# Who rounds the gate, who splits the last weights, and who makes the second products in a quantised feed-forward layer

## The reference, cut to what matters

```python
def act_qdq(x):                       # 16-bit rounding, scale from the largest value
    scale = jnp.maximum(jnp.max(jnp.abs(x)) / 32767, 1e-12)
    return jnp.clip(jnp.round(x / scale), -32768, 32767) * scale
x = act_qdq(x)
up = act_qdq(x @ lpbq_dequant(w_up).T)
gate = act_qdq(x @ lpbq_dequant(w_gate).T)
sig = fixed_qdq_u16(jax.nn.sigmoid(gate))    # round(s * 65536) / 65536
gate = act_qdq(gate * sig)
o = act_qdq(gate * up)
return o @ lpbq_dequant(w_down).T
```

## Time and profile before

| what | us |
|---|---|
| median of 3 runs (lowest, highest) | 802.72 (801.65, 803.15) |
| the profiled execution's own time | 802.26 |
| its span | 800.4 |
| gate matmuls, in the trace | about 541.9 to 613 |
| first loop, until its last product is done | about 614.5 to 683.1 |
| second loop, until its last maximum | about 685.9 to 730.6 |
| down matmuls to the end | about 733.5 to 798 |

### The profile page before, as it was taken

The page is one execution under the profiler, slowest core; times in us unless marked ns, Lnnn a source line. Parts: engine busy times, 40 slices in busy tenths (PEclk is TensorE's granted clock), DMA queues, the critical chain, the costliest instruction groups (busy, mean ns, idle before and its releaser), DMA issues.

```text
span 800.4 us, 11827 instructions
## 1 busy us (share of the span) xinstructions
PE 681.0 (85%) x4160; PEld 462.0 (58%) x4160; DVE 613.7 (77%) x1219; ACT 503.2 (63%) x682; POOL 312.4 (39%) x250
## 2 busy tenths in 40 slices
PE   6882059999999888999999999999998999008998
PEld 5761037988888754566556656564443445004887
DVE  5988866877787388887767675988998899896433
ACT  2235614444553437796896886776665999796983
POOL 4353612566777544233422420002440444694000
PEclk9997559999999999999999999999999999558999
DMA  9937633467634470010013000001100613101343
GB/s 297 339 95 262 194 103 120 122 174 175 146 66 53 107 249 1 2 48 27 1 49 132 1 27 27 27 27 55 78 26 1 237 53 132 52 0 53 113 153 106
DMA packets 59541, 78.68 MB, mean 98 GB/s; under 512 B 7904, under 2 KB 47712, under 8 KB 59488
## 3 DMA queue, kind: packets, MB, share of 16 engines
q1 hardware_dynamic: 49936, 61.10, 23.1%
q0 software_dynamic: 7872, 14.82, 8.5%
q10 hardware_dynamic: 1680, 2.08, 0.8%
HBM read 50.59 MB, written 27.39 MB: 97 GB/s over the span
## 4 chain that ended last, share of the span: by engine, by line
PE 57%; DVE 15%; ACT 13%; issue 4%; POOL 2%; DMA 1%; POOLq 0%; ACTq 0%; DVEq 0%
PE bank L2423 11%; PE bank L2134 8%; PE bank L2190 7%; PE bank L2454 5%; PE bank L1479 4%; PE bank L1513 3%; PE bank L1536 3%; PE bank L1573 3%; PE bank L1533 3%; DVE above L796 2%; PE bank L1494 2%; ACT wgateT L2083 2%; PE bank L1517 2%; DVE high L1914 1%; DVE qx L1208 1%
## 5 line engine op out<-in xcount | busy, mean ns | idle before, releaser
L1334 ACT ACTIVATE x<-bank,bic 128x512 f32<-128x512 f32 x160 | 106.3, 698 | 34.0 <-PE bank L1513 32.6
L1208 DVE TENSOR_REDUCE qx<-bank 128x4 fp32r<-128x616 f32 x128 | 98.2, 797 | 26.9 <-PE bank L1479 25.5
L2134 PE MATMUL bank<-ux,uwh 128*128 128x512 f16 x384 | 92.1, 382 | 0.4 <-ACT ux L2028 0.3
L2134 PEld LDWEIGHTS bank<-ux,uwh 128*128 128x128 f16 x384 | 37.6, 98 | 46.5 <-issue 1.9
L1513 PE MATMUL bank<-qT,K 128*128 128x512 f32 x128 | 61.4, 490 | 3.5 <-ACT x L1334 2.1
L2384 ACT ACTIVATE wgateT<-bank 128x512 f32<-128x512 f32 x32 | 19.2, 600 | 66.1 <-PE bank L2423 66.1
L1479 PE MATMUL bank<-Kb,qTb 128*128 128x308 bf16 x256 | 53.3, 298 | 4.9 <-DVE qx L1208 2.2
L1135 POOL CAST qx<-q 128x1024 fp32r<-128x1024 f32 x8 | 8.5, 1067 | 113.0 <-PE bank L1494 104.0
L2423 PE MATMUL bank<-xh,wh 128*128 128x512 f32 x128 | 50.2, 392 | 0.3 <-DVE xl L2357 0.3
L2134 PE MATMUL bank<-ux,uwl 128*128 128x512 f16 x192 | 50.1, 384 | 0.0
L2423 PE MATMUL bank<-xl,wh 128*128 128x512 f32 x128 | 49.9, 390 | 0.0
(11 more groups left out here) (440 smaller groups left out, 1992.0 us busy)
## 6 DMA issues: line engine op xcount, KB each, us to landing
x_dram<-x SPq DMA_DIRECT2D x4, 1024.0 KB, 5.7
xr<-in_w1T SPq DMA_DIRECT2D x8, 512.0 KB, 4.0
xr<-in_w3T SPq DMA_DIRECT2D x8, 512.0 KB, 4.8
xr<-in_w2T SPq DMA_DIRECT2D x8, 512.0 KB, 6.8
row_dram<-xn SPq DMA_DIRECT2D x8, 512.0 KB, 3.1
x_dram<-xr SPq DMA_DIRECT2D x8, 512.0 KB, 2.9
x<-x_dram SPq DMA_DIRECT2D x8, 512.0 KB, 4.9
xT<-in_xT SPq DMA_DIRECT2D x7, 512.0 KB, 7.3
```

What stands on the lines that cost most here:

```text
L1208: dve.tensor_reduce(qx[:, k, g * GH:(g + 1) * GH, MROW].rearrange("p (u h) -> p u h", u=2), pair[i][:].rearrange("p (u x) -> p u x", u=2)[ ...
L1334: act.activation(pr[g % 2][h], S_[u % 2], ACT.Exp, bias=bic[:, s // 2, h // GH:h // GH + 1]).then_inc(p_done, 1)
L2134: mm = pe.matmul(bank[j][:, m * TB:(m + 1) * TB], w[:, c * HI + cols:c * HI + cols + P], x[:, part, c * TB:(c + 1) * TB], start=(w is uwh ...
```

## The change

Five edits, in the same functions.

1. Of the 24 gate roundings of the first loop, GpSimd now makes 17 (all n from 1 on that are not 1, 5, 9, 13, 17, 21), ScalarE six, VectorE only n = 0. GpSimd issues rounding n + 2 right behind its rounding of sigmoid n, on the condition that product n - 1 is done.
2. GpSimd's rounding of sigmoid n no longer waits for product n - 1, but for product n - 3.
3. The down weights are split by GpSimd alone, in two instructions of 1536 columns near the start of the gate matmuls, into the unused halves of the two weight buffers (`dwh`, `dwl`).
4. In the second loop GpSimd makes twelve products instead of eleven, at places 3, 5, 7, 9, 11, 12, 14, 16, 18, 19, 21, 23; ScalarE rounds the up factor of four of them (7, 12, 18, 23).
5. The three subtractions between these products and ScalarE's copy are gone; TensorE waits for `m_w` = 2 instead of 4, and its down matmuls name `dwh` and `dwl` where they named `uwh` and `uwl` (left out of the diff).

```diff
             with ExitStack() as first:
-                uwh, uwl = (sb(first, f"uw{part}", [P, DC * HI])[:].bitcast(F16)[:, 0:DC * HI] for part in "hl")
+                uw, dw = zip(*((t[:, 0:DC * HI], t[:, DC * HI:2 * DC * HI]) for t in
+                               (sb(first, f"uw{part}", [P, DC * HI])[:].bitcast(F16) for part in "hl")))
+                (uwh, uwl), (dwh, dwl) = uw, dw
                 ux = [sb(first, f"ux{i}", [P, 2 * FW])[:].bitcast(F16)[:, 0:2 * FW].rearrange("p (a w) -> p a w", a=2) for i in range(2)]
...
             ORDER = [s * PAIRS + j for s in DOWN for j in range(PAIRS)]
-            GATES_BY_DVE = (0, 4, 7, 10, 14, 17, 20)
-            POOL_AT = tuple(range(3, FT, 2))
+            GATES_BY_ACT = (1,) + tuple(range(5, FT, 4))
+            GATES_BY_POOL = tuple(n for n in range(1, FT) if n not in GATES_BY_ACT)
+            POOL_AT = (3, 5, 7, 9, 11, 12, 14, 16, 18, 19, 21, 23)
             DVE_AT = tuple(i for i in range(FT) if i not in POOL_AT)
...
             def gates_done(i):
-                return FT - len(GATES_BY_DVE) + sum(k != POOL_AT[0] for k in range(i + 1))
+                return len(GATES_BY_ACT) + sum(k != POOL_AT[0] for k in range(i + 1))
...
                     stored(s)
+                pool.tensor_copy(dwh, wdownT[:].rearrange("p c d -> p (c d)")).then_inc(m_w, 1)
+                pool.wait_ge(m_w, 1)
+                pool.tensor_tensor(dwl, wdownT[:].rearrange("p c d -> p (c d)"), dwh, ALU.subtract).then_inc(m_w, 1)
                 for s in range(2, NS):
...
+                pool.wait_ge(k_gd, 1)
                 for n in range(FT):
                     pool.wait_ge(k_sg, n + 1)
-                    if n >= 1:
-                        pool.wait_ge(k_p, n)
+                    if n >= 3:
+                        pool.wait_ge(k_p, n - 2)
                     pool.tensor_scalar(sq[n % 3], gslot[n], 65536.0, 1.0, ALU.mult, ALU.mult).then_inc(k_sq, 1)
+                    if n + 2 in GATES_BY_POOL:
+                        if n:
+                            pool.wait_ge(k_p, n)
+                        pool.tensor_scalar(gq[(n + 2) % 3], gslot[n + 2], qs[:, 5:6], 1.0, ALU.mult, ALU.mult).then_inc(k_gd, 1)
                     if n % 3 == 0 and n // 3 + 2 < NS:
...
                     pool.tensor_tensor(whole, whole, upper, ALU.mult).then_inc(k_pg, 1)
-                    if k % 3 == 0 and k // 3 < PAIRS:
-                        cols = slice(k // 3 * TB, (k // 3 + 1) * TB)
-                        pool.wait_ge(m_w, 1)
-                        pool.tensor_tensor(uwl[:, cols], wdownT[:].rearrange("p c d -> p (c d)")[:, cols], uwh[:, cols],
-                                           ALU.subtract).then_inc(m_w, 1)
...
-                def gate_integers(n):
-                    if n in GATES_BY_DVE:
-                        if n >= 3:
-                            dve.wait_ge(k_p, n - 2)
-                        else:
-                            dve.wait_ge(y_qs, 2)
-                        dve.tensor_scalar(gq[n % 3], gslot[n], qs[:, 5:6], None, ALU.mult).then_inc(k_gd, 1)
-
                 def minus_product(n):
...
-                gate_integers(0)
+                dve.wait_ge(y_qs, 2)
+                dve.tensor_scalar(gq[0], gslot[0], qs[:, 5:6], None, ALU.mult).then_inc(k_gd, 1)
                 for n in range(FT):
                     largest_up(n)
-                    gate_integers(n + 2)
                     minus_product(n)
...
                 def gate_integers(n):
-                    if n in GATES_BY_DVE:
+                    if n not in GATES_BY_ACT:
                         return
...
                 act.wait_ge(y_qs, 2)
-                gate_integers(0)
                 for n in range(FT):
-                    if n in GATES_BY_DVE:
-                        act.wait_ge(k_gd, GATES_BY_DVE.index(n) + 1)
+                    if n not in GATES_BY_ACT:
+                        act.wait_ge(k_gd, 1 + sum(k <= n for k in GATES_BY_POOL))
                         act.activation(gslot[n], gq[n % 3], ACT.Sigmoid, scale=qs[:, 4:5]).then_inc(k_sg, 1)
...
                         gate_integers(n + 1)
-                    if n not in GATES_BY_DVE:
-                        act.wait_ge(k_gq, sum(k not in GATES_BY_DVE for k in range(n + 1)))
+                    if n in GATES_BY_ACT:
+                        act.wait_ge(k_gq, GATES_BY_ACT.index(n) + 1)
                         act.activation(gslot[n], gq[n % 3], ACT.Sigmoid, scale=qs[:, 4:5]).then_inc(k_sg, 1)
...
                         act.activation(top[:, 1:2], top_gq[:], ACT.Sigmoid, scale=qs[:, 4:5]).then_inc(k_top, 1)
-                act.wait_ge(u_mm, 2 * FT)
-                act.copy(uwh[:], wdownT[:].rearrange("p c d -> p (c d)")).then_inc(m_w, 1)
-
                 act.wait_ge(y_qs, 3)
...
                 spread(2, 2)
-                pe.wait_ge(m_w, 1 + PAIRS)
+                pe.wait_ge(m_w, 2)
                 pe.wait_ge(k_om, FT - 6)
...
```

More of the change, by code:

```diff
@@ L2190, in part @@
                                 mm = pe.matmul(bank[i % 2][:, k * D:(k + 1) * D], o[t % 3][:, m * TB + k * P:m * TB + (k + 1) * P],
-                                               w[:, c * D:(c + 1) * D], start=(o is oh and w is uwh and c == 0 and k % 2 == 0),
+                                               w[:, c * D:(c + 1) * D], start=(o is oh and w is dwh and c == 0 and k % 2 == 0),
                                                stop=(o is ol and c == HIC - 1), skip_group_check=True)
@@ L2199, in ffn_tensor @@
                             for k in range(STEP):
-                                part(oh, (uwh, uwl), k, ms)
+                                part(oh, (dwh, dwl), k, ms)
                         pe.wait_ge(m_l, t + 1)
                         for k in range(STEP):
-                            mm = part(ol, (uwh,), k)
+                            mm = part(ol, (dwh,), k)
                         mm.then_inc(m_t, 1)
@@ L2207, in ffn_tensor @@
                         for k in range(STEP):
-                            part(oh, (uwh, uwl), k)
-                            mm = part(ol, (uwh,), k)
+                            part(oh, (dwh, dwl), k)
+                            mm = part(ol, (dwh,), k)
                             if k % 2:
```

## The result

The changed kernel takes **809.85 us** (median of four runs, 808.45 to 810.79) against 802.54 of before beside it (four runs, 801.65 to 803.15): a ratio of 1.0091, 95% interval 1.0073 to 1.0109. It is slower by 0.9%; 806.9 was predicted (802.3 to 810.8). The profiled execution took 810.13 us with a span of 808.3 and a mean granted clock of 0.930 (before: 802.26, 800.4, 0.936).

What follows compares the result with a forecast made beforehand. The first loop's end was taken as bound by VectorE's product alternating with GpSimd's next sigmoid rounding. Terms +4.3 + 0 + 0 on the profiled 802.26 gave 806.6, plus 0.3 towards the median's level 806.9 us; range 802.3 to 810.8.

Steps and rivals of the forecast that it cites:

- The mechanism: First loop: VectorE's two-SBUF-input product and GpSimd's SBUF-reading roundings exclude each other for whole instructions; product 1.07 us, rounding 0.90 behind the other.
- Rival A: First loop: no exclusion for this product, so the loop ends by TensorE, -4.0 us, 798.3 in all; chance 0.16.
- Rival C: Whole kernel: no change, turn-taking costs 1.3 us and the second loop gives back 1.1, about 802.5; chance 0.04.
- First loop: Gate roundings moved to GpSimd take turns with VectorE's products: +4.3 us, last product ending at 687.4 instead of 683.1.
- The lower bound: First loop, if each hand-over saves what it can: 58.9 us for 22 products, ending at 684.4, +1.3 us.
- The price of a step: First loop: a step with a GpSimd gate rounding takes 0.90 + 1.04 + 1.07 = 3.01 us, 15 such steps.
- the gate rounding with `qs`: GpSimd, first loop: taken as 1.05 us, with half of 0.07 x 15 added on top (0.5 us).
- a step or two: First loop: 0.4 us added for GpSimd putting the next sigmoid in front of a product, 0.75 each.
- Down weights early: Gate matmuls: GpSimd's copy (1.6 us) and subtraction (3.5) stay hidden with 1.0 us to spare, cost 0.
- Second loop: GpSimd has two subtractions fewer and one product more, VectorE one product less: 0, bounds -1.1 and +1.2 us.
- TensorE's clock: Down matmuls: dummies end about 1.1 us sooner; taken as 0, with 2.0 us for one lower-clock visit kept for the range.
- Rival B: First loop: every instruction keeps its full start-to-start time behind the other's end, 3.3 us steps, +9.3, 811.6; chance 0.04.

Runs made afterwards that it cites:

- experiment 1: The changed kernel with the first loop's product reading its second factor from PSUM instead of the rounded sigmoid in SBUF (values meaningless): 797.64 us, ratio to before 0.9928.
- e6: The changed kernel with GpSimd's sigmoid rounding waiting for product n - 1 again, the 17 gate roundings kept: 813.10 us, ratio to before 1.0125.
- e5: The kernel before with only GpSimd's sigmoid rounding relaxed to wait for product n - 3 instead of n - 1: 805.40 us, ratio to before 1.0036.
- e3: The kernel before with only the early down-weight split, its subtractions' removal and twelve second-loop products on GpSimd: 804.02 us, ratio to before 1.0010.
- e2: The kernel before with only GpSimd's 17 gate roundings and the relaxed sigmoid-rounding wait: 808.47 us, ratio to before 1.0069.
- e4: The changed kernel with 34 instead of 28 busy-keeping TensorE matmuls ahead of the last small turn: 808.56 us, ratio to before 1.0068.
- e11: e9 with 34 instead of 28 busy-keeping TensorE matmuls ahead of the last small turn: 802.18 us, ratio to before 0.9984.
- e7: e2 with ScalarE rounding gates 1, 4, ..., 22, those from 4 to 19 as 32-bit integers into PSUM: 802.55 us, ratio to before 0.9994.
- e9: e7 with ScalarE rounding gates 2, 5, ..., 23 too, into SBUF: 801.78 us, ratio to before 0.9988.

## Why the prediction was right, and where its sizes were off

- **The mechanism** (a product with two SBUF inputs and a GpSimd instruction exclude each other): right, and shown by experiment 1, which leaves order, waits and lengths alone. The two durations taken from quite other instructions, 1.07 us for a product behind a rounding and 0.90 for a rounding behind a product, are in the trace to the hundredth (670.11 to 673.19, above). So the rule cited from the Trainium skill (page "SBUF — State Buffer", section "Who interferes with whom") holds for this custom instruction too: 1.96 us at the median beside GpSimd, 1.21 with one factor in PSUM. The second half of that rule, that whoever issues first holds, isn't borne out by the recorded starts: GpSimd's rounding of gate 2 started at 618.47, 0.04 before product 0, and was the one held (2.17 us), as in e6 (664.35, above). Product 0 was to end at 620.9 and ended at 619.74, which cost nothing, as GpSimd then waited for the up piece anyway. Rival A (798.3) is dead; its price was about that of experiment 1, where the exclusion is lifted: 797.6. Rival C (no change) is dead by the loop's +6.3.
- **First loop, +4.3 predicted, +6.3 measured** (within the bounds of +1.3 and +9.3). The lower bound was too low by its own rows: it has seven steps at 1.97 us, where VectorE alone needs 2.26; with 2.26 it is +3.4. The price of a step was right; the gate rounding with `qs` takes 1.11, not 1.05, of which half was put in. Three steps were put in too small. Product 1 was to end at 625.5; it ended at 626.18, held through two roundings of GpSimd:

```profile
623.05 3.13 DVE L1912 CUSTOM_DVE_ANT_0 low<-wgateT,wupT 128x1024 f32<-128x1024 int16 x1 [2.17 <-POOL wupT L1807]
```

```profile
622.97 1.12 POOL L1811 TENSOR_SCALAR wgateT<-low,qs 128x1024 int16<-128x1024 f32 x1
624.05 1.04 POOL L1807 TENSOR_SCALAR wupT<-low 128x1024 uint16<-128x1024 f32 x1
```

  Turn-taking isn't strict: the waiting product was passed over once. With the loop begun 0.4 earlier that is 1.1 of the missing 2.0. The other 0.9 is in the 22 steps behind it, 62.8 us from the end of product 1 to that of product 23 (626.18 to 688.97) against 61.9. Thirteen steps are 2.98 to 3.08, on average 3.05, about as priced (3.01). Two took 3.58 (to product 3) and 3.55 (to product 15), together 1.1 above 3.01; the 0.4 set aside for "a step or two" was the mis-sized term. In the step to product 3 a small instruction with two SBUF inputs of a single column was held too (0.80 us; 0.16 at the same place in before):

```profile
628.58 0.80 DVE L1918 TENSOR_TENSOR peak<-top_gq,top_sq 128x1 f32<-128x1 int16 x1
```

  Product 15 (2.49 us) started during a DMA issue with a rounding right behind it, as in e5. The other seven steps are short (2.28 to 2.30), the number that was predicted, but six of the seven are others than foreseen, and that the count came out is luck. In the pieces without a gate rounding (3, 7, 11, 15, 19, 22) edit 2 lets GpSimd put the next sigmoid in front of the product, so that such a step is as long as one with a gate (the products of 1.91 or 1.92). GpSimd's next gate rounding then has to wait for that product, and the short step comes one piece later.
- **Down weights early, 0:** right. Copy and subtraction took 1.50 and 3.10 and ended at 553.83 (550.73 + 3.10; predicted: cast behind them from 554.7), and GpSimd still waited for ScalarE at 556.32:

```profile
549.14 1.50 POOL L1785 CAST uwh<-wdownT 128x1536 f16<-128x1536 f32 x1
550.73 3.10 POOL L1787 TENSOR_TENSOR uwl<-wdownT,uwh 128x1536 f16<-128x1536 f32 x1
...
556.32 2.13 POOL L1793 TENSOR_TENSOR ux<-xnT,ux 128x1024 f16<-128x1024 f32 x1 [1.51 <-ACT ux L2008]
```

- **Second loop, 0:** right, +0.1. In e3 it is 0.4 longer: 45.91 us from VectorE's first `qs` instruction behind the small turn to `amax`, where before has 45.48 and the changed kernel 45.58.
- **TensorE's clock, 0 with 2.0 kept for the range:** in the profile this is the term that came true at its bound, 0.31 + 1.59 = 1.9 us. The reason given explains about half of the idle time ahead of the turn, which grew from 0.55 to 2.67 us. VectorE's product that is gone lets the busy-keeping matmuls start 1.2 us sooner (10.62 us ahead of `amax` instead of 9.41); but they also took 8.18 us instead of 9.10. In e2, whose second loop is that of before, they took 7.66, and its down product began at the lower level after 1.99 us of idle time. The idle time alone doesn't settle the level either. The profiles of e3 (1.99) and e4 (1.76) began the down product at the lower level and those of before (0.55), e11 (0.81) and e7 (1.05) at the upper; but e5 had only 0.73 and yet a granted clock of 0.52 from 735.4 to 738.0, where its down product begins. Nor is it settled how much of the medians' 7.3 us the clock makes: the first loop takes 6.3 of these by the profile, or 5.7 by the medians of e2 (whose profile has the lower level too), and 1.0 to 1.6 is left for all else.
- **Rival B (3.3 a step)** did not come; steps of 3.18 appear only in e6, where GpSimd's gate rounding is held behind the product and the strict wait is back.

What stays open: which of the two engines goes first when they start within a tenth of a microsecond (in e6 GpSimd's rounding was held 14 times with a lead of 0.04 to 0.06, the product three times behind a lead of 0.05 to 0.08), why a waiting product is sometimes passed over (product 1, but not those of the later steps, which began 0.17 behind the rounding), and what sets TensorE's clock at the down product. None was tried by itself.

## What to carry to other kernels

An idle engine isn't idle capacity: before moving work to GpSimd, look at what VectorE runs beside it, and count every VectorE instruction with two SBUF inputs together with every GpSimd one that reads SBUF as a single queue. A duration beside the other engine, found elsewhere in the trace on quite other instructions, priced one hold here to the hundredth; how many holds there would be, and which, it did not say. If the work must go there, move one input of VectorE's instruction to PSUM first: here that took the time back to that of before (e7, e9), not below it. A stricter wait gave VectorE clean durations and a longer loop (e6), so compare steps, not durations.

## What was not expected of the hardware

- The loss could be turned into a gain only by where one operand lies: 809.85 with both factors in SBUF, 797.64 with one in PSUM (experiment 1, which does not use the rounded sigmoids).
- A product was held 3.13 us, through two instructions of GpSimd in a row (changed kernel; 3.14 in e7), so the worst hold isn't one instruction.
- Relaxing a wait made a kernel slower (e5, 1.0036): with the strict wait for product n - 1 no product of the kernel before was held (1.21 to 1.23), without it four were.
- VectorE's rounding with one input and 16-bit output is held too. It takes 0.75 us with GpSimd at rest (the first one of the loop, before) and 1.18 to 1.40 where a rounding of GpSimd has 0.6 to 0.9 us left (before, e5); it then ends 0.55 us behind that rounding. VectorE's maximum, with one input as well, is not held (1.21).
